# Folding a causal long convolution's transforms round the middle of the sequence, and putting one short convolution on TensorE

## The reference, cut to what matters

```python
up = (u @ w_in + b_in).transpose(0, 2, 1)              # u: layer norm of x, (16, 256, 128)
uc = conv1d(up, sf_w, taps=3, causal, per channel) + sf_b
x0, x1, v = jnp.split(uc, 3, axis=1)                   # x0 is the gate
k = _implicit_filter(...).T                            # a filter of 256 values per channel
v = v * x1
n = 2 * l                                              # 512
y = jnp.fft.irfft(jnp.fft.rfft(v, n=n) * jnp.fft.rfft(k, n=n), n=n)[..., :l]
v = y + v * filt_bias[None, :, None]
out = (v * x0).transpose(0, 2, 1)
return out @ w_out + b_out
```

## Time and profile before

| what | value |
|---|---|
| median of 3 runs | 515.03 us (514.41 to 516.46) |
| time of the profiled execution | 516.48 us |
| its span, first to last instruction | 514.6 us |
| PE busy | 471.2 us (92%) |
| DVE busy | 364.7 us (71%) |
| POOL busy | 327.0 us (64%) |
| ACT busy | 270.8 us (53%) |
| chain that ended last, by engine | PE 74%, DVE 10%, ACT 8% |

### The profile page before, as it was taken

How to read it: one execution, slowest core, us unless ns; L and a number is a source line. 1 busy time by engine, 2 the same in 40 slices (tenths; PEclk the granted TensorE clock), 3 DMA queues, 4 the chain that set the end, 5 groups by cost and what they waited for, 6 DMA issues and landing times.

```text
span 514.6 us, 13024 instructions
## 1 busy us (share of the span) xinstructions
PE 471.2 (92%) x3852; PEld 367.3 (71%) x3852; DVE 364.7 (71%) x1136; ACT 270.8 (53%) x716; POOL 327.0 (64%) x446
## 2 busy tenths in 40 slices
PE   3989999999899999996899999999889999999994
PEld 1658878787665999974576676666677656999962
DVE  6688999967766656544877787878877766566635
ACT  3464444653561555544667676676765542555530
POOL 4455766648772466651798899999746771566640
PEclk9999999998999999999999999999979999999997
DMA  8999950001111233316000000000001111333229
GB/s 280 325 383 406 403 225 1 0 2 41 48 54 47 73 85 95 84 52 165 0 3 3 2 3 2 4 1 3 2 14 36 53 53 47 84 83 95 78 73 291
DMA packets 36993, 47.56 MB, mean 92 GB/s; under 512 B 4186, under 2 KB 28123, under 8 KB 36798
## 3 DMA queue, kind: packets, MB, share of 16 engines
q1 hardware_dynamic: 31648, 35.90, 21.4%
q0 software_dynamic: 4544, 9.35, 5.3%
q10 hardware_dynamic: 734, 1.50, 1.0%
HBM read 17.86 MB, written 28.87 MB: 91 GB/s over the span
## 4 chain that ended last, share of the span: by engine, by line
PE 74%; DVE 10%; ACT 8%; issue 5%; POOL 1%; DMA 0%; ACTq 0%; DVEq 0%; POOLq 0%
PE bank L783 69%; ACT silu_sh L1249 2%; PE bank L305 2%; PE bank L893 2%; DVE prod L1614 2%; ACT rows L1242 1%; ACT scores_odd L1224 1%; ACT wide L1224 1%; DVE conv_xv L1521 1%; ACT k_tok L1224 1%; PE bank L1179 1%; PE bank L795 1%; DVE residual L1620 1%; DVE prod L1791 1%; PE bank L992 1%
## 5 line engine op out<-in xcount | busy, mean ns | idle before, releaser
L660 POOL DMA_INDIRECT routed<-row_out,row_token x78 | 74.9, 960 | 66.4 <-DVE row_token L1682 49.9
L783 PE MATMUL bank<-row_in_t,row_weights 128*128 128x128 f32 x624 | 84.0, 278 | 1.9 <-issue 1.2
L783 PEld LDWEIGHTS bank<-row_in_t,row_weights 128*128 128x128 f32 x624 | 75.7, 192 | 4.2 <-issue 2.8
L651 POOL DMA_INDIRECT sorted_rows<-rows,place x64 | 62.3, 973 | 23.0 <-issue 14.3
L1290 ACT ACTIVATE row_silu<-bank 128x256 f32<-128x256 f32 x78 | 29.9, 383 | 48.2 <-PE bank L783 48.2
L1674 DVE TENSOR_SCALAR row_weights<-experts 128x512 f32 x78 | 33.9, 435 | 26.9 <-issue 23.2
L783 PE MATMUL bank<-wide,weights_sb 128*128 128x512 f32 x112 | 51.5, 597 | 0.0
L783 PE MATMUL bank<-experts,row_act 128*128 x312 | 50.1, 283 | 1.3 <-ACT row_out L1224 1.1
L1249 ACT ACTIVATE silu_sh<-bank 128x512 f32<-128x512 f32 x32 | 19.0, 594 | 60.0 <-PE bank L783 59.8
L1666 DVE TENSOR_TENSOR row_act<-row_silu,bank 128x256 f32<-128x256 f32 x78 | 32.8, 420 | 19.8 <-ACT row_silu L1290 10.9
L1224 ACT ACTIVATE wide<-bank 128x512 f32<-128x512 f32 x54 | 29.4, 592 | 30.8 <-PE bank L783 17.1
(11 more groups left out here) (194 smaller groups left out, 1092.2 us busy)
## 6 DMA issues: line engine op xcount, KB each, us to landing
sorted_rows<-zeros SPq DMA_DIRECT2D x1, 17028.0 KB, 50.6
row_in<-sorted_rows SPq DMA_DIRECT2D x78, 64.5 KB
rows<-routed SPq DMA_DIRECT2D x8, 256.0 KB, 4.9
scores_odd<-routed SPq DMA_DIRECT2D x8, 256.0 KB, 5.3
out<-residual SPq DMA_DIRECT2D x8, 256.0 KB, 3.6
routed<-row_out,row_token POOLq DMA_INDIRECT x78, 2.3
tables_sb<-tables SPq DMA_DIRECT2D x1, 1024.0 KB, 8.8
experts<-rt_gate SPq DMA_DIRECT2D x1, 1024.0 KB, 18.4
```

The costliest lines, as they stand in the source:

```text
L651: pool.indirect_dma_start(sorted_rows, bass.IndirectOffsetOnAxis(ap=place[:, t:t + 1].bitcast(U32), axis=0), rows[:, t, :], None).then_inc ...
L660: pool.indirect_dma_start(routed, bass.IndirectOffsetOnAxis(ap=row_token[:, r:r + 1].bitcast(U32), axis=0), row_out[:, r, :], None).then_i ...
L783: return pe.matmul(out_, lhsT, rhs, start=start, stop=stop, **kw)
```

## The change

The tables are centred on the middle of the sequence (t - 127.5). A cosine is then even and a sine odd about the middle, so the sequence is folded once, into first half plus mirrored second half and first half minus it; the cosines need only the sum, the sines only the difference, each of 128 times. POOL makes the two halves in `value`, behind the product. `inverse` gives an even part and an odd part of 128 times each, and `gate` unfolds them: ACT copies the odd part out of PSUM (`copy_odd`), DVE adds and subtracts, then multiplies with the gate from SBUF. The filter's own transform keeps the old tables.

From pair 2 on (`BY_MATMUL` = 2) the gate third's short convolution is three matmuls in `project`, with `w_in` scaled by each tap and the input shifted by 0, 1 and 2 columns. DVE keeps only the edge correction of that third. Its scaled weights are made once (`scale_gate_weights`), from taps that one more transfer brings in on ACT's queue, ahead of the last table. The transfer of the folded tables is of the same size as that of the old inverse table; `forward(0)` waits for it now. In round 7 ACT's `keep(2)` and `scale_rows(1)` stand ahead of `copy_odd(7)`.

```diff
+    centred = np.arange(P)[:, None] - (L - 1) / 2
+    fold_cos, fold_sin = np.cos(2 * np.pi * centred * f / NF), -np.sin(2 * np.pi * centred * f / NF)
+    fold_sin[:, 0] = -np.sin(np.pi * centred[:, 0])
...
             def value(k):
                 pool.wait_ge(c_conv, 3 * k + 2)
+                pool.tensor_tensor(value_c[:], conv_xv[:, 0, :], conv_xv[:, 1, :], ALU.mult).then_inc(c_value, 1)
+                pool.wait_ge(c_value, k + 1)
                 wait(pool, c_value_turned, k)
-                pool.tensor_tensor(value_c[:], conv_xv[:, 0, :], conv_xv[:, 1, :], ALU.mult).then_inc(c_value, 1)
+                v = value_c[:].rearrange("p (b t) -> p b t", b=2)
+                folded = value_fold.rearrange("p (b h t) -> p b h t", b=2, h=2)
+                for h, op in enumerate((ALU.add, ALU.subtract)):
+                    pool.tensor_tensor(folded[:, :, h, :], v[:, :, 0:P], v[:, :, L - 1:P - 1:-1], op).then_inc(c_folded, 1)
...
                 for n, g in enumerate(THIRDS):
                     wait(pe, c_conv, 3 * (k - 1) + n + 1)
-                    mm(pe, bank[1 + g][:], w_in_sb[:, g * D:(g + 1) * D], normed_t[:]).then_inc(c_proj, 1)
+                    if g or k < BY_MATMUL:
+                        mm(pe, bank[1 + g][:], w_in_sb[:, g * D:(g + 1) * D], normed_t[:]).then_inc(c_proj, 1)
+                        continue
...
+                    for late in range(3):
+                        last = mm(pe, o[:, :, late:L], gate_weights[:, 2 - late, :], n_t[:, :, 0:L - late],
+                                  start=(late == 0), stop=(late == 2), skip_group_check=True)
+                    last.then_inc(c_proj, 1)
...
             def forward(k):
...
-                        for s in range(SB):
-                            last = mm(pe, o, dft[:, s, c, f * P:(f + 1) * P], v[:, s, :, :],
-                                      start=(s == 0), stop=(s == SB - 1))
+                        last = mm(pe, o, fold_dft[:, c, f * P:(f + 1) * P], v[:, c, :, :])
...
             def inverse(k):
...
-                            last = mm(pe, bank[6][:, b * L:(b + 1) * L], y[:, c, f, b, :], inverse_dft[:, c, f, :],
-                                      start=(c == 0 and f == 0), stop=(c == 1 and f == FB - 1))
+                            last = mm(pe, bank[6][:, b * L + c * P:b * L + (c + 1) * P], y[:, c, f, b, :],
+                                      inverse_dft[:, c, f, :], start=(f == 0), stop=(f == FB - 1))
...
+            def copy_odd(k):
+                act.wait_ge(c_inverse, k + 1)
+                copy(act, out_odd, bank[6][:].rearrange("p (b h t) -> p b h t", b=2, h=2)[:, :, 1, :]).then_inc(c_odd_copied, 1)
...
-                       (2, each(tap2)), (3, each(conv_apply)), (3, each(copy_normed)),
+                       (2, each(tap2)), (0, beside({7: third_keep})), (0, each(copy_odd)), (3, each(conv_apply)),
+                       (3, each(copy_normed)),
...
+            def scale_gate_weights():
+                dve.wait_ge(gate_taps_loaded, 16)
+                dve.tensor_tensor(gate_weights, w_in_sb[:, 0:D].unsqueeze(1).to_broadcast([P, 3, D]),
+                                  gate_tap_rows.rearrange("p (k d) -> p k d", k=3), ALU.mult).then_inc(gate_weights_made, 1)
...
             def gate(k):
-                dve.wait_ge(c_inverse, k + 1)
+                dve.wait_ge(c_odd_copied, k + 1)
+                even = bank[6][:].rearrange("p (b h t) -> p b h t", b=2, h=2)[:, :, 0, :]
+                y = out_c.rearrange("p (b t) -> p b t", b=2)
+                dve.tensor_tensor(y[:, :, 0:P], even, out_odd, ALU.add).then_inc(c_unfolded, 1)
+                dve.tensor_tensor(y[:, :, L - 1:P - 1:-1], even, out_odd, ALU.subtract).then_inc(c_unfolded, 1)
+                dve.wait_ge(c_unfolded, 2 * (k + 1))
                 wait(dve, c_out, k)
-                dve.tensor_tensor(gated[:], bank[6][:], gates[:, bass.ds(k * PT, PT)], ALU.mult).then_inc(c_gated, 1)
+                dve.tensor_tensor(gated[:], out_c, gates[:, bass.ds(k * PT, PT)], ALU.mult).then_inc(c_gated, 1)
```

More of the change, by code:

```diff
@@ L140, in hybrid_block @@
 def hybrid_block(nc, x, weights, filter_weights, f_w1, filt_bias, b_out, rt_gate, rt_up, rt_down,
-                 tables, positions, out):
+                 tables, positions, gate_taps, out):
     with ExitStack() as ctx:
@@ L172, in hybrid_block @@
         dft = table("dft", "p (t c f) -> p t c f", t=TAU, c=2)
+        fold_dft = table("fold_dft", "p (c f) -> p c f", c=2)
         inverse_dft = table("inverse_dft", "p (c f t) -> p c f t", c=2, f=FB)
@@ L320, in hybrid_block @@
         value_c = sb("value_c", [P, PT])
+        scores_odd = sb("scores_odd", [P, 2 * HEADS * P])
+        value_fold = scores_odd[:, 0:PT]
+        out_odd = scores_odd[:, PT:PT + 2 * P].rearrange("p (b t) -> p b t", b=2)
+        out_c = scores_odd[:, 2 * PT:3 * PT]
+        gate_tap_rows = scores_odd[:, 3 * PT:3 * PT + 3 * D]
+        gate_weights = scores_odd[:, 4 * PT:4 * PT + 3 * D].rearrange("p (k d) -> p k d", k=3)
         value_t = sb("value_t", [P, PAIR, D])
@@ L336, in hybrid_block @@
         c_value = sem("c_value")
+        c_folded = sem("c_folded")
+        c_odd_copied = sem("c_odd_copied")
+        c_unfolded = sem("c_unfolded")
+        gate_taps_loaded = sem("gate_taps_loaded")
+        gate_weights_made = sem("gate_weights_made")
         c_value_turned = sem("c_value_turned")
@@ L522, in hybrid_block @@
         v_wide = sb("v_wide", [P, 3, AT, V_N])
-        scores_odd = sb("scores_odd", [P, AT * HEADS * P])
         scores = [s.rearrange("p (t h q) -> p t h q", t=AT, h=HEADS)
@@ L984, in project @@
                     wait(pe, c_conv, 3 * (k - 1) + n + 1)
-                    mm(pe, bank[1 + g][:], w_in_sb[:, g * D:(g + 1) * D], normed_t[:]).then_inc(c_proj, 1)
+                    if g or k < BY_MATMUL:
+                        mm(pe, bank[1 + g][:], w_in_sb[:, g * D:(g + 1) * D], normed_t[:]).then_inc(c_proj, 1)
+                        continue
+                    if k == BY_MATMUL:
+                        pe.wait_ge(gate_weights_made, 1)
+                    o, n_t = (a[:].rearrange("p (b t) -> p b t", b=2) for a in (bank[1], normed_t))
+                    for late in range(3):
+                        last = mm(pe, o[:, :, late:L], gate_weights[:, 2 - late, :], n_t[:, :, 0:L - late],
+                                  start=(late == 0), stop=(late == 2), skip_group_check=True)
+                    last.then_inc(c_proj, 1)
             def turn_value(k):
-                pe.wait_ge(c_value, k + 1)
+                pe.wait_ge(c_folded, 2 * (k + 1))
                 pe.wait_ge(ln_c.copied, min(k + 2, PAIRS))
                 for j in range(PAIR):
-                    last = pe.transpose(bank[0][:, j * P:(j + 1) * P], value_c[:, j * P:(j + 1) * P], ident)
+                    last = pe.transpose(bank[0][:, j * P:(j + 1) * P], value_fold[:, j * P:(j + 1) * P], ident)
                 last.then_inc(c_value_turned, 1)
@@ L1360, in tap2 @@
                     act.activation(dst, bank[1 + g][:], ACT.Identity, bias=conv_bias[:, g:g + 1],
-                                   scale=taps[:, g, 2:3]).then_inc(c_tap2, 1)
+                                   scale=taps[:, g, 2:3] if g or k < BY_MATMUL else 1.0).then_inc(c_tap2, 1)
             silu_table, keep, scale_rows, silu_half, pairs, row_tiles = experts_act(act, 0)
@@ L1847, in _ @@
             short_conv(0)
+            scale_gate_weights()
             pipelined([(3, each(conv_stats_in)), (2, each(short_conv)), (0, beside({6: first_choice, 7: third_choice})),
@@ L1988 @@
 THIRDS = (1, 2, 0)
+BY_MATMUL = 2
 EDGE_STEPS = 7
@@ L2023 @@
         "rt_gate": L0_ffn_rt_gate, "rt_up": L0_ffn_rt_up, "rt_down": L0_ffn_rt_down,
-        "tables": tables, "positions": positions}
+        "tables": tables, "positions": positions,
+        "gate_taps": np.asarray(L0_attn_a_sf_w)[0:D].reshape(D, -1).T.reshape(-1)}
     arrays = {name: np.ascontiguousarray(a) for name, a in arrays.items()}
```

29 lines of the change are left out of this document (20 added, 9 removed).

## The result

The changed kernel takes 513.47 us (median of 20 runs), beside 516.7 us for the kernel before (20 runs): a ratio of 0.9942, 95% interval 0.9927 to 0.9957. It is faster by 3.0 us, where 6.0 were forecast, and the time lies above the predicted range. The forecast of 509.0 us stood on a median of 515.03 us from 3 runs; the 20 runs of the kernel before put it at 516.7, so 1.7 of the 4.5 us by which the median missed belong to that level and not to the change. The runs of the changed kernel are not spread evenly: ten took 509.6 to 512.6 us at a mean granted clock of PE (the share of its full speed that it was given, over the whole execution) of 0.971 to 0.983, and ten took 514.3 to 516.0 us at 0.964 to 0.968. The profiled execution, 515.37 us with a span of 513.6 us and a clock of 0.967, is of the second kind; before it was 0.981.

A forecast was written before the change was run, and what follows sets the result against it. PE bound the rounds at 11.33 us, DVE next at 11.18; afterwards DVE at 10.98. Gains of 5.7 to 7.1 us over start, rounds and tail, 6.0 taken, gave 509.0 us median; 8-in-10 range 505.3 to 512.8 us.

The forecast's parts named there:

- DVE's round: One convolution round on DVE: 11.18 us less 1.45 plus 0.77 gives 10.50 us, or 10.98 with a 0.48 us wait.
- The block: In DVE's round, the gate product (two SBUF inputs) waits 0.48 us until POOL's v times x1 is over.
- ending with POOL's v times x1: Sign in the trace: gate's product takes about 1.1 us instead of 0.68 and ends with that POOL instruction.
- POOL: right: POOL's round: two foldings at 0.73 us each, 1.46 together; sum 10.8 us, narrowly under DVE's 10.98.
- Rival 2: POOL becomes the bound: backward reading costs 1.27 us a folding, POOL's round 11.5 to 11.9 us, total 512 us; chance 0.17.
- PE's terms: PE's round: inverse and forward fall from 3.45 to 1.73 us each, project gains 1.72; sum 9.60 us instead of 11.33.
- Round 0: First convolution round on DVE: starts 34.75, gate(0) waits for copy_odd(0) at 40.05, ends 46.4 instead of 47.00 us; gain 0.6.
- Rounds 1 to 5: Rounds 1 to 4 gain 0.35 us each, 1.4 together; round 5 gains 1.2, ending at 100.4 us, 3.2 gained in all.
- The tail: Rounds 6 and 7: three transforms lose 1.73 us each; 7.1 us gained in all, 5.7 if half clock costs 1.4.
- Rival 3: Tail gain given back: ACT's table, scaling and copies behind copy_odd(6) leave 3 us of gain, 512 us; chance 0.10.
- The sum: Whole execution: 5.7 to 7.1 us gained, 6.0 taken; 516.5 falls to 510.5 us profiled, 509.0 median; row stage onward moves whole.
- Rival 4: PE's clock falls in the rounds because PE idles 1.4 us in each; slower, 518 us; chance 0.07.

## Why the prediction was wrong

- **DVE's round: right, with a small error of size.** The prediction put it at 10.98 us blocked and 10.50 free; 10.62 and 10.18 were measured. The block was forecast as 0.48 us and is 0.44. The missing 0.36 us lay mostly in the 11.18 that it started from. From one start to the next, the four products of frequencies took 2.57 us before and 2.40 after; the edge correction of the gate third took 0.19 and now 0.07, since the instruction behind it no longer needs it; the rest is in pieces of under 0.05. That the products paused for PE before is argued, not shown. The sign "ending with POOL's v times x1" was at odds with the sum, which had the product start there; it ended 0.55 us later.
- **POOL: right.** Two foldings took 1.41 us together when nothing was in their way (1.46 forecast) and 1.75 behind DVE's product. Rival 2 is out; reading backwards costs nothing extra.
- **PE's terms: right.** 16 records of `inverse` at 1.95 us, 8 of `forward` at 1.89, 6 of the gate third at 2.73; from one start to the next 1.78 us (1.73 forecast), 1.72 and 2.57 for `project` (4.30 forecast). The windows count PE busy for 10.18 us of a round where the sum had 9.60; as the ends of matmuls are modelled, which of them is nearer stays open.
- **Round 0: the step that failed first.** "First foldings 33.0, `turn_value(1)` 33.5, `project(2)` with its two more matmuls 37.75, `inverse(0)` 39.6": the wait was in the walk, since PE had nothing to do from 30 us on, but every matmul behind it was priced at full clock. `inverse(0)` began at 39.67 and `forward(1)` at 41.45, and `conv_stats_in(4)` at 48.15 instead of 46.4. Filling the wait gave 1.23 of these 1.75 us back; the rest probably goes with DVE's edge corrections waiting for POOL (one took 0.82 us, at 38.84), for which 0.2 us had been charged in another place.
- **Rounds 1 to 5:** the shorter rounds made this good; 3.00 us gained at their end, 3.2 forecast. That these are so near each other is luck: 1.75 us too many at the start against 0.36 too few in each round.
- **The tail: the step that failed most.** "After the change PE waits there longer, so I expect it again; with `up_half(0, 0)` behind it, it costs 1.4 us." It was expected, and its size taken from before, where one `inverse` had been hit. After, the wait came earlier, before `gate(1)`, so that `gate(1)`, `project_out(6)`, a turn, `gate(2)`, `inverse(7)` and `up_half(0, 0)` all ran at half clock for most of their length, 3.3 us, and a further stretch at 128 us cost 1.7: 5.0 us instead of 1.4. In the second profile of the same kernel it was 1.0, so the term is no single number, and 1.4 lies between what the two executions show. With the clock held the tail gave 19.48 - 16.04 = 3.4 us (`inverse(6)` to `project_out(7)`, which began at 103.31 us before), where 7.1 - 3.2 = 3.9 had been forecast. Part of both is the low clock of the kernel before: with that filled too, the same stretch took 121.11 - 103.14 = 17.97 us before, so at full clock on both sides the change is worth 1.9 us in the tail, of the 5.2 that the three transforms shed. Rival 3, which gave the tail nothing even at full clock, is out in that strict form; that ACT's new order takes much of the rest is not ruled out.
- **The sum.** With the clock whole in start and tail, and the start's wait filled, an execution took 509.82 us: 6.7 us under the profiled one of before. So with the clock kept the change was worth about the 7.1 us that the prediction gave for that case. In the profiled execution the clock was mis-sized by 3.6 us in the tail and left out at the start, 1.2 us. Together that is 4.8 us, and the profiled execution (515.37) missed 510.5 by 4.9; the other errors about cancel: 1.8 us from five rounds of 0.36 on one side; on the other 0.5 each of the start and the tail, and 0.8 lost behind the row stage, which the prediction had move as a whole (this execution was 7.4 us ahead there and 6.7 at the end). The forecast's median of 509.0 us is met only by the better executions: ten of 20 took 509.6 to 512.6 us.
- **Rival 4** had the right cause in the wrong place. It looked for a low clock in the rounds, where PE's waits are short and the clock stayed at 1.00, and not at the two places with waits of over 2 us. With the folding alone, whose rounds have waits of up to 2.33 us, it came in the rounds too. The Trainium skill says that idling brings the throttle back (TensorE: Matmul & The Clock Gate, Part 1); both places agree. No row explains why the wait of 2.20 us was not followed by it every time.

What stays open: why the same wait of 2.20 us in the tail lowered the clock in the profiled executions of four kernels (the changed one twice, the folding alone, the one with the product from PSUM, the one with `keep(1)` first, there 2.12 us) and not in two (idle matmuls at the start, project first). The start's wait of 2.7 to 3.5 us lowered it in all five profiled executions that had it. The stretch at 122 to 130 us was at a low clock in four of the fourteen profiled executions (the changed kernel, the tail filled, both filled, `keep(1)` first), though all have a wait of 1.2 to 1.3 us there; nothing was put into that wait, so what a filling would give there is untested. That the runs' split into two groups comes from the stretches in start and tail is inferred from their mean clocks, not seen in a trace of each; the clock also fell in later places that the change does not touch.

## What to carry to other kernels

Where a change takes work off TensorE, walk it through start and tail for every wait that it makes or moves (here 2.2 and 3.45 us), and price all matmuls behind that wait at half clock as well as at full, as two ends of a range and not as one term; an engine that is no longer the bound can lose more there than it gained. Put real work into such a wait by swapping two steps of the order, or else idle matmuls into a bank that nobody reads. Price the same stretch of the kernel before in the same way, or its own low clock is counted as gain. And sum an engine's own round from starts, piece by piece: small pauses and dependences may leave with the change.

## What the runs showed of the hardware

- A wait of PE of 2.7 to 3.5 us at the start was followed by half clock in five of five profiled executions, one of 2.1 to 2.2 us in the tail in five of seven. A wait of 3.06 us for ACT at 229 to 249 us, which every kernel has, the one before too, was followed by a lower clock in 13 of 14; the exception is the kernel before with its tail filled.
- Where a wait of over 2 us was filled, with idle matmuls or real work, the clock right behind it stayed at 1.00 in every profiled execution (two, and four with project first, at the start; four in the tail). The changed kernel's 20 times span 6.4 us, before's 3.6.
- A DVE instruction of 4 columns with two inputs in SBUF took 0.75 to 1.12 us instead of 0.15 when POOL was busy with a 128x512 one.
- POOL made two foldings of 128x256, one of them reading backwards, in 1.41 us, where one forward instruction of that shape took 0.73.
